# Dense experts whose downward product keeps the weights in place and sums eight experts in one bank

## What is computed

```python
scores = sigmoid(xf @ gate_w.T); sel = top_k(scores + expert_bias, 2)
for e in range(8):
    w_t = sum(where(sel == e, top_scores, 0), -1)       # one gate per token and expert
    h = square(relu((xf * w_t[:, None]) @ w_up[e].T))   # 128 -> 256
    out += h @ w_down[e].T                              # 256 -> 128
x = x + 0.5 * out
```

## Time and profile before

| what | us |
|---|---|
| median of 3 runs (lowest, highest) | 2848.12 (2844.03, 2848.57) |
| the profiled execution | 2866.33 |
| its span, first to last instruction | 2864.2 |
| PE busy in the span | 2597.2 |
| DVE, ACT, POOL busy in the span | 2070.6, 1913.6, 1673.6 |
| the two dense stages together | about 465 |

### The profile page before, as it was taken

One profiled execution on the slowest core, in us unless ns is written; L12 is line 12 of the kernel. 1 busy time (PEld: TensorE's weight loads), 2 busy tenths in 40 slices (PEclk: granted clock), 3 DMA queues, 4 the chain that ended last, 5 costly groups with the idle time before them and its releaser, 6 DMA issues. The chain is left out here.

```text
span 2864.2 us, 51642 instructions
## 1 busy us (share of the span) xinstructions
PE 2597.2 (91%) x18932; PEld 1774.7 (62%) x18932; DVE 2070.6 (72%) x4694; ACT 1913.6 (67%) x4049; POOL 1673.6 (58%) x836
## 2 busy tenths in 40 slices
PE   7999999999999999998998286999999999998286
PEld 6996555555555565646887176565665666665176
DVE  5677888888888889885776633778778778776632
ACT  5665777687777777776775143878778778776143
POOL 0002989898989889893110176656556556555077
PEclk9999999999999999998999598999999999999588
DMA  3014554454544454540001244000000000000133
GB/s 107 1 60 111 120 122 120 114 139 112 133 113 120 119 130 113 122 101 16 20 17 27 69 89 67 1 2 9 9 2 9 9 2 9 9 2 9 40 80 51
DMA packets 144649, 179.21 MB, mean 63 GB/s; under 512 B 30547, under 2 KB 74128, under 8 KB 143888
## 3 DMA queue, kind: packets, MB, share of 16 engines
q1 hardware_dynamic: 130320, 165.20, 22.8%
q0 software_dynamic: 14080, 10.73, 2.8%
HBM read 56.51 MB, written 17.72 MB: 26 GB/s over the span
## 5 line engine op out<-in xcount | busy, mean ns | idle before, releaser
L2047 POOL TENSOR_TENSOR arena<-arena 128x2048 f32<-128x2048 f32 x192 | 882.0, 4595 | 216.9 <-ACT arena L1353 200.3
L1658 DVE TENSOR_REDUCE top<-psum 128x1 f32<-128x512 f32 x1024 | 649.4, 683 | 79.5 <-PE psum L937 79.4
L937 PE MATMUL psum<-stack 98*128 98x512 f32 (+1 forms) x2048 | 604.8, 423 | 15.6 <-ACT arena L1353 9.3
L1353 ACT ACTIVATE arena<-psum 128x512 f32<-128x512 f32 x1024 | 546.6, 599 | 48.1 <-PE psum L937 47.7
L1008 PE MATMUL psum<-arena,values 128*32 128x512 f32 (+1 forms) x3072 | 484.5, 603 | 3.5 <-ACT arena L1353 2.6
L937 PEld LDWEIGHTS psum<-stack 98*128 98x128 f32 (+1 forms) x2048 | 357.1, 191 | 210.3 <-DVE top L1658 87.5
L2057 POOL TENSOR_TENSOR by_query<-by_query,row_tables 128x1024 f32<-128x1024 f32 x170 | 321.7, 1900 | 217.1 <-DVE row_tables L1664 215.9
L1656 DVE TENSOR_REDUCE row_tables<-psum 128x1 f32<-128x512 f32 x512 | 335.6, 679 | 2.7 <-PE psum L945 1.7
L1008 PEld LDWEIGHTS psum<-arena,values 128*32 128x32 f32 (+1 forms) x3072 | 128.6, 119 | 276.7 <-issue 252.2
L1676 DVE COPY arena<-psum 128x512 f32<-128x512 f32 x256 | 175.7, 689 | 120.4 <-PE psum L989 119.4
L2017 POOL TENSOR_SCALAR rstd<-mv 128x4 f32<-128x4 f32 x56 | 13.2, 235 | 415.6 <-DVE mv L1522 413.2
(11 more groups left out here) (208 smaller groups left out, 4685.1 us busy)
## 6 DMA issues: line engine op xcount, KB each, us to landing
stack<-halves SPq DMA_DIRECT2D x768, 128.0 KB, 2.4
qk_ring<-qk_split SPq DMA_DIRECT2D x64, 256.0 KB, 2.9
v_ring<-v_split SPq DMA_DIRECT2D x32, 256.0 KB, 3.0
tokens<-xn SPq DMA_DIRECT2D x16, 256.0 KB, 2.4
arena<-in_wg SPq DMA_DIRECT2D x16, 256.0 KB
arena<-in_wu SPq DMA_DIRECT2D x16, 256.0 KB
arena<-in_wd SPq DMA_DIRECT2D x16, 256.0 KB
wqkv<-in_w_qkv SPq DMA_DIRECT2D x2, 1536.0 KB, 9.1
```

What stands on the lines that cost most here:

```text
L937: return T_.matmul(bk, st[0:k, side, h, cols], st[0:k, 1 - side, h, :], start=True, stop=True)
L1353: S_.activation(prob[tile % N_PROB][:, h, :], psum[:, bank[key], :], ACT.Exp, scale=scale).then_inc(released[bank[key]], 1)
L1658: give(V_.reduce_max(top[i][:, j:j + 1], psum[:, bank[key], :], AX.X), key)
L2047: G_.tensor_tensor(to, old, prob[tile % N_PROB], ALU.add).then_inc(summed, 1)
```

## The change

In batches 1 to 7 of the first dense stage and 2 to 7 of the second ("wide" batches, 13 in all, 104 experts), the downward product turns round: the downward weights are stationary and the hidden activations move, 512 tokens at a time. Products of the first half of the hidden units are made in three rounded products, those of the second half in one product in full fp32; all eight experts add up in one bank (4). The result is transposed: it has features on the partitions. After the eighth expert ACT copies the bank, PE transposes it back in four tiles, and DVE adds it to x in one instruction (`collect0`).

Tokens now lie along the free axis, so that the gate can no longer be one number per partition. It becomes a row that is repeated over all 128 partitions: PE transposes the gates of a batch (`spread0`), ACT copies them, SP stores 16 KB to DRAM and then loads, for each expert, one row of 512 gates into 128 partitions (256 KB). DVE multiplies both upward banks with it in place (relu and gate in one instruction), ACT squares out of PSUM three times (rounded and full first half, full second half), and DVE takes the low half. The upward products run three experts ahead in place of one, in all batches. The downward weights are split once per stage (`split0`). SP now takes part in `compute0`, with a load per expert. The hidden tiles, gate rows and low weights lie in three slots each.

```diff
-RANK = 0.4
+RANK = 0.3
+DEPTH = 3
+WIDE_FROM = (1, 2)
+WIDE_LEAD = 0.7
-            ready = here - 2 * step
+            ready = here - 2 * step - (WIDE_LEAD if wide(s, b) else 0)
+            if wide(s, b):
+                stream("spread0", (s, b), 1, 1, ready, ready)
+                collect = here + EXPERT_ROUNDS + step / 2
+                stream("collect0", (s, b), 1, 1, collect, collect)
             if routed:
-                stream("route", (0, b), 6, 6, here + EXPERT_ROUNDS, here + 1.85 * EXPERT_ROUNDS)
-                stream("route", (0, b), 11, 11, here + 1.85 * EXPERT_ROUNDS, here + 2.4 * EXPERT_ROUNDS)
+                stream("route", (0, b), 6, 6, here + EXPERT_ROUNDS + step, here + 1.45 * EXPERT_ROUNDS)
+                stream("route", (0, b), 11, 11, here + 1.45 * EXPERT_ROUNDS, here + 2.0 * EXPERT_ROUNDS)
...
 PE
+                def down_wide(e):
+                    pe.wait_ge(hidden_split, wide_group(s, b, e) + 1)
+                    for k, (w, m) in enumerate(((highs, high), (highs, low), (lows, high))):
+                        T_.matmul(bk, w[:, at, 0, :], m[:, 0, :], start=(e, k) == (0, 0), stop=False)
+                    pe.wait_ge(*read(("up", s, b, e, 1)))
+                    ins = T_.matmul(bk, down_w[s][half][:, at, 1, :], hidden_full[s][i][:, 1, :], start=False,
+                                    stop=e == EXPERTS - 1)
+                    ins.then_inc(expert_added, 1)
+            def spread0(s, b):
+                pe.wait_ge(gates_ranked, s * BATCHES + b + 1)
+                T_.matmul(bk[0:TILES_B * EXPERTS, 0:P], gate_weight[b % 2]..., ident, is_transpose=True)
+            def collect0(s, b):
+                pe.wait_ge(*read(("acc", s, b)))
+                turn(bk, [collected[:, t, :] for t in range(TILES_B)]).then_inc(done, 1)
...
 ACT
+                def up_wide(b, e):
+                    if hidden_free(s, b, e):
+                        act.wait_ge(*hidden_free(s, b, e))     # the downward product three experts back
+                    act.wait_ge(hidden_scaled, 2 * group + 1)
+                    S_.activation(high[:, 0, :], psum[:, bank[first], :], ACT.Square)
+                    S_.activation(full[:, 0, :], psum[:, bank[first], :], ACT.Square)
+                    act.wait_ge(hidden_scaled, 2 * group + 2)
+                    S_.activation(full[:, 1, :], psum[:, bank[second], :], ACT.Square)
...
 DVE
+                def up_wide(b, e):
+                    dve.wait_ge(*share_loaded(s, b, e))
+                    for c in range(2):
+                        tick(V_.scalar_tensor_tensor(out=products, in0=products, scalar=0.0, in1=share,
+                                                     op0=ALU.max, op1=ALU.mult), hidden_scaled)
+                def split_hidden(b, e):
+                    dve.wait_ge(*read(("up", s, b, e, 0)))
+                    tick(V_.tensor_tensor(low, full, high.bitcast(fp32), ALU.subtract), hidden_split)
+            def collect0(s, b):
+                x_done[b] = give(V_.scalar_tensor_tensor(out=X[:, here, :], in0=psum[...], scalar=0.5, in1=X[...]))
...
 SP
+            def spread0(s, b):
+                sp.wait_ge(*read(("shares", s, b)))
+                Y_.dma_start(shares[s * BATCHES + b]..., share_rows[s][...]).then_inc(shares_stored, 16)
+                def load_share(b, e):                          # in call 2e+1 of compute0, four experts ahead
+                    if group >= N_HIDDEN:
+                        sp.wait_ge(hidden_scaled, 2 * (group - N_HIDDEN) + 2)
+                    sp.wait_ge(shares_stored, 16 * (wide_batch(s, b) + 1))
+                    load(share_wide[s][group % N_HIDDEN], shares[s * BATCHES + b, e].partition_broadcast(P), ...)
```

More of the change, by code:

```diff
@@ L236, in __init__ @@
         self.moments, self.xn, self.xt = Ring(range(3)), Ring(range(2)), Ring(range(3))
-        parts = dict(prepare0=self.prepare0, compute0=self.compute0, route=self.route,
+        parts = dict(prepare0=self.prepare0, compute0=self.compute0, spread0=self.spread0,
+                     collect0=self.collect0, route=self.route,
                      project=self.project, maxima=self.maxima, rows=self.rows, probs=self.probabilities,
@@ L286, in compute0 @@
         if b == 0:
-            up(0, 0)
+            for e in range(DEPTH):
+                up(0, e)
             yield
@@ L292, in compute0, with spread0, collect0 @@
                 yield
-            self.once(self.products, ("down", s, b, e))
-            yield
+            if not wide(s, b):
+                self.once(self.products, ("down", s, b, e))
+            elif e == 0:
+                self.mixed.take(("acc", s, b))
+            elif e == EXPERTS - 1:
+                self.mixed.give(("acc", s, b))
+            yield
+    def spread0(self, s, b):
+        self.once(self.other, ("shares", s, b))
+        yield
+    def collect0(self, s, b):
+        self.once(self.other, ("down", s, b, EXPERTS - 1))
+        yield
     def project(self, l, n):
@@ L801, in arena_free @@
         def arena_free(l):
-            return read(("narrow", 0, EXPERTS - 1, 1)) if l else read(("down", 0, BATCHES - 1, EXPERTS - 1))
+            return read(("narrow", 0, EXPERTS - 1, 1)) if l else expert_done(0, BATCHES - 1, EXPERTS - 1)
         def region_free(s):
@@ L1162, in experts1 @@
                 yield
-            play(order, dict(prepare0=prepare0, route=route, ahead=ahead, compute0=compute0, project=project,
+            play(order, dict(prepare0=prepare0, route=route, ahead=ahead, compute0=compute0, spread0=spread0,
+                             collect0=collect0, project=project,
                              maxima=maxima, rows=rows_of_maxima, probs=probabilities, turns=turns, last=last_tiles, sums=sums_of,
@@ L1621, in compute0, with split0 @@
                     if following(b, e):
-                        up(*following(b, e))
+                        if wide(s, following(b, e)[0]):
+                            up_wide(*following(b, e))
                         yield
-                    down(e)
+                        if not wide(s, following(b, e)[0]):
+                            up(*following(b, e))
+                    if not wide(s, b):
+                        down(e)
+                    split = following(b, e, DEPTH - 1)
+                    if split and wide(s, split[0]):
+                        split_hidden(*split)
+                    yield
+            def collect0(s, b):
+                key, here = ("down", s, b, EXPERTS - 1), slice(b * TILES_B, (b + 1) * TILES_B)
+                dve.wait_ge(*written(key))
+                dve.wait_ge(*x_done[b])
+                x_done[b] = give(V_.scalar_tensor_tensor(
+                    out=X[:, here, :], in0=psum[:, bank[key], :].rearrange("p (t d) -> p t d", t=TILES_B), scalar=0.5,
+                    in1=X[:, here, :], op0=ALU.mult, op1=ALU.add), key)
+                yield
+            def split0(s):
+                dve.wait_ge(got_down, 32 * (s + 1))
+                for i in range(4):
+                    cols = slice(i % 2 * SEQ, i % 2 * SEQ + SEQ)
+                    dve.wait_ge(down_rounded, 4 * s + i + 1)
+                    tick(V_.tensor_tensor(down_halves[s][1][i // 2][:, cols], weights0[s][1 + i // 2][:, cols],
+                                          down_halves[s][0][i // 2][:, cols].bitcast(fp32), ALU.subtract), down_split)
                     yield
@@ L2126, in load0, with spread0, compute0 @@
                 yield
+            def spread0(s, b):
+                sp.wait_ge(*read(("shares", s, b)))
+                Y_.dma_start(shares[s * BATCHES + b].rearrange("e (t q) -> (e t) q", t=TILES_B),
+                             share_rows[s][0:TILES_B * EXPERTS, :]).then_inc(shares_stored, 16)
+                yield
+            def compute0(s, b):
+                def load_share(b, e):
+                    group = wide_group(s, b, e)
+                    if group >= N_HIDDEN:
+                        sp.wait_ge(hidden_scaled, 2 * (group - N_HIDDEN) + 2)
+                    if s:
+                        sp.wait_ge(*written(("out", 0, BATCHES - 1)))
+                    sp.wait_ge(shares_stored, 16 * (wide_batch(s, b) + 1))
+                    load(share_wide[s][group % N_HIDDEN], shares[s * BATCHES + b, e].partition_broadcast(P),
+                         share_in[group % N_HIDDEN])
+                if b == 0:
+                    yield
+                for e in range(EXPERTS):
+                    if following(b, e):
+                        later = following(b, e, DEPTH + 1)
+                        if later and wide(s, later[0]):
+                            load_share(*later)
+                        yield
+                    yield
             def load_attention(l):
```

159 lines of the change are left out of this document (141 added, 18 removed).

## The result

| kernel | median us | runs | ratio to before (95% interval) |
|---|---|---|---|
| before | 2848.12 | 7 | 1 |
| after | 2865.26 | 7 | 1.0075 (1.0063 to 1.0088) |

What follows compares the result with a forecast made beforehand. PE's own work was taken to bound the first stage and, with a ring of hand-offs close under it, the second. Terms -6 + 3.5 + 15 = +12.5 us on the 2848.1 median gave 2861 us, range 2836 to 2877.

Steps and rivals of the forecast that it cites:

- the ring: Second stage: new closed chain of hand-offs between engines, 33.0 us per batch (31.5 to 34.7) against 29.9 before.
- PE per expert: Wide batches: PE saves 0.16 us per expert, net about 0.8 per batch after added transposes; -6 us in the first stage.
- The burst: First stage: gate loads queue on SP behind six stores of split attention weights, costing 3.5 us once (0 to 6).
- the links: Second stage: steps from gate row through DVE, POOL, ACT, PE and SP, plus hand-offs, summing to 32.0 us per batch.
- the clock: Second stage: PE partly at half speed behind a 3.6 us pause, lengthening each turn by 1.0 us (0.9 to 2.7).
- The table load: ACT's table switch in the second stage: taken as 1.28 us; the skill's 2.66 would make the ring 33.4.
- the rival of a clock that stays low: Second stage: clock falls at every pause and stays down through D2, turns of 34.7, 2870 us; chance 0.15.
- The end: End of the second stage: copy and transposition back before the moments, +1.1 us, against 0.8 for PE's cheaper last batch.
- the pause in batch 1: Second stage, batch 1: the pause there goes with the deeper lead, 1.0 us gained.
- The slack ring: Rival: gates come early enough, PE sets the second stage's pace with turns of 28.7, 2836 us; chance 0.18.
- The shorter ring: Rival: second-stage steps overlap more, turns of 30.5 in place of 33.0, no change at 2850 us; chance 0.20.
- The costlier PE product: Rival: full-width fp32 product takes 1.0 us or more, nothing saved on PE, 2867 us; chance 0.03.

Runs made afterwards that it cites:

- e2: Changed kernel with no wide batch in either stage, only upward products three experts ahead and the lists around them; 2835.84 us, 0.9968 of before.
- e1: Changed kernel with wide batches in the first dense stage alone, the second narrow, upward products three ahead; 2837.70 us, 0.9975 of before.
- e5: Changed kernel plus 24 useless PE transposes ahead of each router transpose of the second stage; 2854.34 us, 1.0029 of before.
- e7: Changed kernel with the six stores of the attention's split weights issued in three pairs instead of one burst; 2865.21 us, 1.0062 of before.
- e8: e2 with the lead of the upward products set back from three experts to one; 2853.36 us, 1.0023 of before.
- e4: Changed kernel with the second stage's routing steps spread later on the lists, entries moved only; 2840.83 us, 0.9980 of before.
- e3: Changed kernel with gate rows loaded from input x, without waiting for the stored gates; 2858.88 us, 1.0048 of before.
- e12: Changed kernel with wide form in the second stage alone, routing steps late as in e4, gate rows from x; 2842.38 us, 0.9979 of before.

## Why the prediction was right, and where it wasn't

The direction and the mechanism are right, and the time is near: 2865 against 2861, 17 to 21 us of loss against 12.5. But part of the agreement is luck, since in both stages errors cancel, and a turn of the ring was left out.

*PE per expert.* Forecast 0.16 saved, measured 0.24; net per batch 1.3 in place of 0.8. Bound and choice were for the fp32 product; the whole expert came out 0.08 below the sum. *The burst* was sized at 3.5 and cost 6.3, just outside its 0 to 6: the term for the wait was near (4.04), but the half-speed clock behind it (2.2) wasn't in it, though the same rule was applied in the second stage. The two misses cancel, and the stage came out at -2.3 against -2.5. By the experiments most of it is not the wide form's doing: the narrow form with the lead has -1.4 (e2), and e1 is only 0.3 below e2.

*The ring.* Five turns were costed at 15.4 us over before in all. The first five measured turns take 1533.50 - 1368.50 = 165.0 us, before 149.75: +15.3. The turns that start at full clock are 32.0, the same number as the sum of the links, but that is a coincidence: each of them ends with the upward group at half speed, 2.24 us from its start to the logits (1531.26 to 1533.50) where full clock takes 1.52 (1434.94 to 1436.46). Without these 0.7 the links sum to 31.2, and in e5, where no clock was low, turns are 31.0. So the links were forecast 0.8 to 1.0 too long and the clock 0.5 too short, and the two nearly cancel: 33.0 forecast, 32.5 measured on average. The links themselves, from DVE's timeline (gate row to moments), POOL's and ACT's:

```profile
1515.67 1.30 DVE L1805 SCALAR_TENSOR_TENSOR psum<-psum,arena 128x512 f32<-128x512 f32 x2 [1.65 <-DMA arena<-shares]
...
1524.38 0.68 DVE L1836 SCALAR_TENSOR_TENSOR X<-psum,X 128x512 f32<-128x512 f32 x1
1525.10 0.87 DVE L1686 BATCH_NORM_STATS2 stats<-X 128x6 f32<-128x128 f32 x4
1525.89 0.36 DVE L1689 BATCH_NORM_AGGREGATE mv<-stats 128x2 f32<-128x6 f32 x4
```
```profile
1526.34 0.58 POOL L2241 TENSOR_SCALAR rstd<-mv 128x4 f32<-128x4 f32 x1 [25.43 <-DVE mv L1689]
...
1528.50 0.55 POOL L2247 TENSOR_SCALAR shift<-shift 128x4 f32<-128x4 f32 x1
```
```profile
1504.30 0.60 ACT L1406 ACTIVATE hidden_high<-psum 128x512 fp32r<-128x512 f32 x1 [2.81 <-PE psum L996]
1504.80 0.59 ACT L1407 ACTIVATE arena<-psum 128x512 f32<-128x512 f32 x1
1505.28 0.60 ACT L1409 ACTIVATE arena<-psum 128x512 f32<-128x512 f32 x1
1505.90 1.28 ACT L1372 ACT_TABLE_LOAD   x1
1507.19 0.23 ACT L1372 ACTIVATE r_score<-r_value 128x32 f32<-128x32 f32 x1
```

DVE 1515.67 to 1526.25, 10.6 (forecast 10.9); POOL 1526.34 to 1529.05, 2.7 (2.0, so +0.7); three squares 1.58 from the first start to the last end (1.85 for a group, three times in the ring: -0.8). From the end of ACT's copy of the gates to the row it is 5.1 (1510.55 to 1515.67; 4.7): the gate's load lands in 3.5 to 3.6 in place of 2.9, its store in about 1.4 in place of 1.8.

```profile
arena<-shares SPq DMA_DIRECT2D x104, 256.0 KB, 3.5
```

What the named links don't account for is in ACT's other steps and in the hand-offs, each a little shorter than its row. *The table load* takes 1.28 us, begins 0.02 after the last square ends (1505.88), and the next ACTIVATE starts behind it at once. The price of a switch with a drain that the Trainium skill gives (ScalarE: Activation LUTs, "What ACT_TABLE_LOAD costs") is not borne out here: the turn of 33.4 that it would have given is met only where the clock fell.

*The clock.* 1.0 us a turn was taken and e5 measured 1.5. Half speed followed the pauses of 3.86, 3.75, 3.56 and 3.40 us, not those of 2.95 and 3.26, and in e7 not one of 3.48. The rule of the Trainium skill (TensorE: Matmul & The Clock Gate, "HAM oscillation — how this bites in real kernels"), by which every turn begins cold, holds in four of six turns, and both the forecast and the rival of a clock that stays low have a part in the result.

*The step that failed: a turn too few.* The sum counted the turns between the gates of batch 2 and those of batch 7. The ring is passed once more, by batch 7's own experts: its first gate row comes late like all others (DVE waits 3.71 us at 1549.29), PE pauses 3.40, and the clock is at half for 10.2 us. In before that turn is the shortest, 27.7, since no `prepare0` is left; after, 33.4. That is +5.8 where the sum had nothing. In e7, with the same code in this stage and half speed for only 1.7 us behind this pause, the turn is 30.5: some 3 of the 5.8 us are the ring, and the rest goes with this execution's clock. The end came out at +1.4 (forecast +1.1 - 0.8), the pause in batch 1 at -0.5 (-1.0). So 15.3 + 5.8 + 1.4 - 0.5 = 22.0, which is the 21.9 of the table, against 15.

*The term that was not seen: the lead.* The deeper lead was valued at 1.0 us, for the pause in batch 1. It is worth 9 us against before (e2), and 16 where it alone is changed (e2 against e8). The prediction even named the 1.3 us pauses as the reserve of the second stage, but as something that the ring replaces. In the changed kernel the gain is hidden: the ring takes it and more. That is why the sum of the change's visible parts came out near while the account of its causes was incomplete: the rest of the change costs about 29 us, not 17, and the lead gives 9 back. The prediction also put the whole loss on the ring's new links; that 24 of the 29 us go when the routing entries are moved back (e4) is nowhere in it.

*The rivals.* The slack ring (2836) is what the list order of e4 makes of the kernel: 2840.8. Its condition was met by moving entries, and its forecast turn, 28.7, was met within 0.3. The shorter ring (30.5) was nearer than it looks: at full clock turns are 31.0 (e5), and only the clock brings them to 32.0 and more. The costlier PE product is refuted by the period of 2.94.

## What to carry to other kernels

When a change adds a way through DRAM and new steps on several engines, write down the closed chain from buffer to buffer with its links from the trace, compare its sum with the present period, and count how often it is passed, the last time included. Then look whether the order of the list can put independent work of the busiest engine into the chain's longest wait: here this was worth 24 us with no instruction changed, largely by undoing a move that the change itself had made. And take a change apart before judging it: without its wide batches, with a lead of two or three experts, the kernel was 0.2 to 0.3% faster, and the rest of the change lost three times as much. Last, when an experiment takes a link out, look in its trace whether the link is gone: e3 and e12 took out 1.1 us of a way of 5.

## What the runs showed of the hardware that was not expected

- POOL's small instructions on 128x4 took 0.58, 0.30 and 0.55 us where they stood beside DVE's 128x512 operations with two operands, against 0.23, 0.20 and 0.24 in the last turn of after (1586.21), where DVE stood still. The traces show the coincidence, no run isolated it.
- Three ACT squares of 128x512 out of PSUM start 0.48 to 0.50 us apart (1504.30, 1504.80, 1505.28), though each is recorded as 0.60.
- The granted clock doesn't follow from the length of the last pause alone: e12 has a stretch of 3.4 us at half speed at a pause of 2.09 us, after has none behind 3.26 and e7 none behind 3.48. And TensorE that is given useless work in its pauses was faster by 11 us in all.
- The first attention, the same code in all kernels, took between 1058.5 us (e2) and 1069.9 us (e3) from entry to end. A single profiled execution can't show a difference of 10 us in the whole; stage times and medians can.
